# Layer 1 of a fused two-layer kernel: the scaling, shifting and query product of the second half's memory rows move from GpSimd to VectorE, with their operand in a PSUM bank

## The reference, cut to what matters

```
q = l2n(x @ Wq.T);  k = l2n(x @ Wk.T);  v = ln(x @ Wv.T) * vn_g + vn_b
b = sigmoid(xc @ ig_w.T + ig_b) * k * v         # xc: a short convolution of x, through silu
mem[t] = gamma[t] * mem[t-1] + b[t]             # along the tokens
out = (ln(mem) * mn_g + mn_b) * q               # per head     <- the lines that the change moves
o = ln(out) * gn_g + gn_b
y = (o * sigmoid(xc @ og_w.T + og_b)) @ Wo.T
x = x + y + ternary_ffn(x)
```

## Time and profile before

| | |
|---|---|
| median of 3 runs | 904.14 us (903.02 to 904.34) |
| the profiled execution | 904.06 us, of which the span from first to last instruction is 902.3 us |
| TensorE busy (PE) | 752.3 us, 83% of the span |
| VectorE busy (DVE) | 647.4 us, 72% |
| ScalarE busy (ACT) | 451.5 us, 50% |
| GpSimd busy (POOL) | 411.1 us, 46% |
| mean granted TensorE clock | 0.939 of full speed |

### The profile page before, as it was taken

How to read it: one execution, slowest core, us unless ns; L and a number is a source line. 1 busy time by engine, 2 the same in 40 slices (tenths; PEclk the granted TensorE clock), 3 DMA queues, 4 the chain that set the end, 5 groups by cost and what they waited for, 6 DMA issues and landing times. The chain is left out here.

```text
span 902.3 us, 15623 instructions
## 1 busy us (share of the span) xinstructions
PE 752.3 (83%) x5602; PEld 645.9 (72%) x5602; DVE 647.4 (72%) x1146; ACT 451.5 (50%) x717; POOL 411.1 (46%) x335
## 2 busy tenths in 40 slices
PE   3268889999999999999999999990888588595843
PEld 3257678888888888888888888880667376484642
DVE  6998976787777767767777776634548949859765
ACT  4256545655655655655655655553534325335300
POOL 2244542343366585485254254334171743824721
PEclk9999998999999999999999999995889889699785
DMA  5011210210001101101000000004000000000000
GB/s 156 22 42 45 85 36 25 55 37 20 19 21 43 43 20 49 42 20 27 19 3 20 20 3 19 3 1 153 1 1 1 1 24 0 0 23 0 0 23 24
DMA packets 21383, 25.82 MB, mean 29 GB/s; under 512 B 4418, under 2 KB 17090, under 8 KB 21060
## 3 DMA queue, kind: packets, MB, share of 16 engines
q1 hardware_dynamic: 21316, 24.93, 9.4%
HBM read 14.83 MB, written 3.28 MB: 20 GB/s over the span
## 5 line engine op out<-in xcount | busy, mean ns | idle before, releaser
L593 DVE TENSOR_REDUCE neg_max<-s_pair 128x4 f32<-128x1024 f32 x127 | 155.0, 1220 | 80.9 <-PE s_pair L805 80.7
L446 ACT ACTIVATE probs<-t_pair 128x1024 f32<-128x1024 f32 x128 | 131.2, 1025 | 139.5 <-PE t_pair L830 139.1
L345 POOL TENSOR_TENSOR hid<-g,hid 128x512 f32<-128x512 f32 x64 | 82.2, 1284 | 185.5 <-DVE g L704 144.2
L339 POOL TENSOR_TENSOR hid_lo<-hid,hid_hi 128x512 fp32r<-128x512 f32 x64 | 85.8, 1340 | 96.6 <-ACT hid_hi L456 96.5
L805 PE MATMUL s_pair<-K,Q 96*128 96x256 f32 x508 | 85.1, 291 | 15.1 <-DVE neg_max L593 9.7
L805 PEld LDWEIGHTS s_pair<-K,Q 96*128 96x128 f32 x508 | 76.0, 195 | 23.8 <-issue 8.1
L830 PE MATMUL t_pair<-Q,K 104*128 104x512 f32 x256 | 85.6, 416 | 0.3 <-DMA Q<-max_parts 0.3
L872 PE MATMUL down<-w_hi,hid_hi 128*128 128x256 f32 x256 | 83.9, 328 | 0.7 <-POOL hid_lo L339 0.7
L872 PE MATMUL down<-w_lo,hid_hi 128*128 128x256 f32 x256 | 72.1, 282 | 0.0
L872 PE MATMUL down<-w_hi,hid_lo 128*128 128x256 f32 x256 | 72.1, 282 | 0.0
L845 PE MATMUL misc<-probs,V 128*32 128x256 f32 x1024 | 69.6, 390 | 2.0 <-DVE a_mem L570 1.0
(11 more groups left out here) (249 smaller groups left out, 1984.4 us busy)
## 6 DMA issues: line engine op xcount, KB each, us to landing
stage<-in_ternary SPq DMA_DIRECT2D x18, 256.0 KB, 2.8
Q<-q_hi SPq DMA_DIRECT2D x64, 64.0 KB, 2.0
stage<-in_scales SPq DMA_DIRECT2D x8, 384.0 KB, 3.4
X<-in_x SPq DMA_DIRECT2D x8, 256.0 KB, 3.8
Q<-q_lo SPq DMA_DIRECT2D x32, 64.0 KB, 2.0
Q<-max_parts SPq DMA_DIRECT2D x128, 4.0 KB
out<-res SPq DMA_DIRECT2D x8, 256.0 KB, 2.2
shared<-in_l1w SPq DMA_DIRECT2D x1, 1536.0 KB, 6.1
```

The lines of the kernel that those rows point to most:

```text
L339: pool.tensor_tensor(hid_lo[:, m % 2, :, :].rearrange("p a n -> p (a n)"), hid[:, m % 2, :], hid_hi[:, m % 2, :, :].rearrange("p a n -> p ...
L345: pool.tensor_tensor(hid[:, m % 2, :], g[:, m % 2, :], hid[:, m % 2, :], ALU.mult).then_inc(S["hid_done"], 1)
L446: act.activation(probs[:, u % 2, th, :], t_pair[:], ACT.Exp, scale=SCALE).then_inc(S["probs_done"], 1)
L593: dve.tensor_reduce(neg_max[:, u % 2, 4 * jp:4 * jp + 4], score_banks(u, jp)[:].rearrange("p (s n) -> p s n", n=SEQ), AX_X, ALU.max, negat ...
```

## The change

```
@@ memory_scaled: the operand of half 1 is bank 5, no longer `o` in SBUF
-            y = o[:, pair(b), :] if b else turned(banks[4][:])
+            y = turned(banks[4 + b][:])
             inc(linked(engine, wait, f"op_link{b}", [
                 (heads(y), heads(y), mn_g, ALU.mult),
                 (heads(y), heads(y), mn_b, ALU.add),
@@ the queue of GpSimd
-                if late is not None:
-                    memory_scaled(pool, late, 1)
@@ memory_normed: the normed half 1 is written to bank 5 in place
-                        inc(dve.tensor_tensor(heads(o[:, pair(b), :] if b else y), heads(y), each(sm[:, b, :]), ALU.mult), "mn_done")
+                        inc(dve.tensor_tensor(heads(y), heads(y), each(sm[:, b, :]), ALU.mult), "mn_done")
@@ the queue of VectorE
                 if late is not None:
                     memory_scaled(dve, late, 0)
+                    memory_scaled(dve, late, 1)
                 if early is not None:
                     hidden_low(dve, early, 0)
```

## The result

The changed kernel takes 914.87 us (median of 4 runs, 913.95 to 915.72), the kernel before 904.24 beside it; the ratio is 1.012 with a 95% interval of 1.0103 to 1.0138. Forecast were 909.8 us and a range of 906.2 to 912.4. The sign was right, and the cost is nearly twice the forecast one. Timed again later beside other kernels, it took 914.98 us against 904.16.

What follows compares the result with a forecast made beforehand. VectorE's full queue up to `hidden(4)` was taken as the bound: +1.60 us in each of three turns (4.80) plus 0.90 in the last, +5.7 on 904.14, gave 909.8 us (0.6% slower), range 906.2 to 912.4.

Steps and rivals of the forecast that it cites:

- The path: VectorE full up to `hidden(4)`: three added operations cost 2.07 us a turn, net +1.60; GpSimd's relief directly worth zero.
- The credits: On VectorE in the loop's turns, `hidden_low(0)` (L1167) gains 0.09 us and L1508 of half 0 gains 0.38, unstretched by GpSimd.
- The second rival: GpSimd doesn't cause VectorE's stretch, or another of its operations takes the place: no credit, +8.3 us, 912.4 us; chance 0.10.
- The rule that the prediction took: GpSimd shares SBUF interfaces with VectorE; two-SBUF-input instructions contend, so credits are due and the moved operations safe from stretch.
- The last turn: Late part alone, VectorE on the chain to the second `gated`: +2.07 less gains of 1.06 and 0.11, sum +0.90 us.
- The step that failed: On VectorE, L1508 of half 1 stays stretched by GpSimd's `values` of half 0, which moves along; no change counted.
- the two signs of being wrong: VectorE idle between the scans and `hidden(4)`, or `ffn_up(5)` at clock 1.00 in two turns or more.
- The fall of the clock itself: Gap before `ffn_up(3)` grows from 1.54 to 3.1 us; if it then runs slow, it ends 1.8 us later still, off the path.
- The clock behind `hidden(4)`: TensorE's clock effect on the turn's end: zero in the sum, bounds -1.8 and about +0.9 us a turn.
- The first rival: Low clock moves from `ffn_up(5)` to `ffn_up(3)`: -1.8 us a turn; whole 904.4 us, 0.06; one or two turns, 0.18.
- The third rival: TensorE takes over before `hidden(4)`, up to +0.9 us a turn: 911.2 us; chance 0.08.
- the fourth: Rival: freed GpSimd shortens the convolution; price 0, 909.8 us, its chance inside the forecast's 0.58.

Runs made afterwards that it cites:

- e4: The kernel before without the three operations of half 1 on any engine, so the relief of GpSimd alone: 902.07 us (0.9979).
- f3: The changed kernel without the four operations of `values` of half 0 on GpSimd and the waits for it: 907.56 us (1.0038).
- f4: The changed kernel with half 1 kept in bank 5 down to `gated`, centring included: 907.07 us (1.0043).
- e2: The changed kernel with eight extra matmuls on TensorE filling the gap before `ffn_up(3)`: 910.97 us (1.0079).
- e1: The changed kernel with `hidden(2)` moved ahead of the three operations of half 1 on VectorE: 915.39 us (1.0123).
- h1: The changed kernel again, unaltered, timed beside other kernels: 914.98 us (1.0119).
- f2: The kernel before with eight extra matmuls ahead of `ffn_up(3)` and twelve ahead of `ffn_up(5)`: 900.22 us (0.9959).
- g1: The kernel before, bank 6 products of `ffn_up` waiting for ScalarE alone, with four filling matmuls ahead of `ffn_up(3)` and eight ahead of `ffn_up(5)`: 900.40 us (0.995).
- e3: The kernel before with three same-shaped operations more on VectorE, on bank 5, GpSimd keeping its own: 916.27 us (1.0143).
- f1: The changed kernel with eight extra matmuls ahead of `ffn_up(3)` and twelve ahead of `ffn_up(5)`: 905.45 us (1.0009).
- g2: The changed kernel with the split waits and filling of g1 and half 1 centred in bank 5 as in f4: 902.23 us (0.9972).

## Why the prediction was right or wrong

**The path.** Right. VectorE is full between the scans and `hidden(4)` in the changed kernel too, the three operations went on the path whole, and GpSimd's relief was worth nothing directly. In every turn `hidden(3)` came 1.60 us later, the forecast's figure.

**The credits.** Right. L1167 and L1508 of half 0 fell to 0.68 and 0.69 us; e4 has them without the addition. The second rival (no credit, 912.4 us) fell by this, though its price lay nearer to the time. Its clause that another of GpSimd's operations may take the place points the right way, but it was priced at the credited operations alone. The rule that the prediction took from the Trainium skill, "GPSIMD Engine Reference", section "Specifications", agrees with f3 (0.69 us with GpSimd idle) and f4 (0.70 us with one input in a bank).

**The last turn.** Right on VectorE (0.88 us later at the second `gated`, for 0.90), and within 0.15 us at the end of the span (0.75).

**The step that failed** is in the same paragraph as the credits: "L1508 of half 1 is stretched by `values` of half 0, which is not touched and moves along, so I leave it." It didn't move along. `values` of half 0 hangs on the convolution, that on ScalarE's sigmoid behind `ffn_up(3)`, and `ffn_up(3)` lost its clock: GpSimd's operation came 2.7 to 2.9 us later in the turn where VectorE's came 1.6 later. The relative shift of 1.1 to 1.3 us put other pairs side by side, at 1.0 to 1.15 us a turn, 3.2 in all. e2 takes away the low clock and the 3.2 us go with it. Neither of the two signs of being wrong that the prediction named came up: VectorE had no idle time between the scans and `hidden(4)`, and `ffn_up(5)` stayed at the low clock. A busy queue doesn't show that operations in it have grown longer.

The fall of the clock itself had been foreseen, gap of 3.1 us included. Its price was looked for in two places only, at `ffn_up(5)` and in TensorE being late itself, and the chain over ScalarE and GpSimd to the contention was missed, although the same prediction gave credit for contention at another place.

**The clock behind `hidden(4)`** was taken at zero, with bounds of -1.8 (`ffn_up(5)` fast) and +0.9 a turn (TensorE late before it). It was +0.3 to +0.6, 1.4 in all, by a third way: the low clock lasted longer behind `ffn_up(5)`. The first rival (the fast clock moves to `ffn_up(5)`) fell: the gap there was 4.0 to 4.5 us and not 1.5. The stretched operations made `hidden(4)` 1.0 to 1.15 us later still; the low clock delayed `ffn_up(3)` by 1.4 us and not by 1.8; and in the third and fourth turns the products from `gamma(0)` to `gate(1)` took 8.3 to 8.4 us in place of 9.3 to 9.5. Where the stretch was all but absent and `ffn_up(3)` slow (two turns each of f3 and f4), the gap did shrink, to 2.3 us, and `ffn_up(5)` was slow all the same. In e1 and e2 the gap was 3.6 us or more. The third rival (TensorE late) fell by the same gaps. For the fourth, GpSimd idled 9.41 us ahead of the convolution, which came later and not earlier.

**Outside the turns** 1.3 us of the profiled pair weren't forecast. Of these 0.9 lie ahead of the first scan, which is at 680.6 to 684.2 us over the thirteen profiles, with the same code of layer 0 in all; it is at 681.4 in the changed kernel's second profile (h1) and at 680.6 in f4, so this is no effect of the change. The other 0.4 us is found in every run of the kernels with the longer queue, as the last section shows; its cause is open.

The range ended at 912.4, its upper end being a rival that failed. It should have carried the cost of the contention moving.

## What to carry to other kernels

When work is added to a full queue, list what else shifts, and by how much against it: here VectorE's queue behind the addition moved by 1.6 us and GpSimd's `values` by 2.8, and the contention that came of it cost two thirds of the forecast 1.6 us again. A wait of TensorE that is lengthened (here from 1.54 to 3.13 us) should be priced along all that hangs on the matmuls behind it, not at the next critical one alone; filling it with throw-away matmuls is a cheap test, and filling both waits is here also a gain (4 us on the kernel before). A two-input operation of VectorE next to a busy GpSimd wasn't stretched where one of its inputs was in PSUM (f4).

## What the runs showed of the hardware

- An operation with both tensor inputs in SBUF was held up until GpSimd's running instruction was nearly done, whatever its own size: 64 elements took 0.97 us for 0.23, 512 took 1.84 for 0.69. Take from the end of a stretched operation its plain duration, and that of GpSimd's instruction stands 0.14 us behind. L1506 in the second turn: 717.46 + 1.69 - 0.69 = 718.46, and GpSimd's pair ended at 718.60. The small product there: 720.57 + 0.97 - 0.23 = 721.31, and 721.45. L1508 of before: 777.18 + 1.48 - 0.69 = 777.97, and 778.11. From the first scan on, the thirteen profiles have 82 stretched operations (by 0.06 us or more) of four kinds: L1167, the product of k with its norm, the centring and the small product. For all of them the distance is 0.12 to 0.15 us. So the size of a stretch can be read off where the two timelines overlap.
- GpSimd waits as well: where the product was under way first, GpSimd's pair took 3.05 to 3.09 us in place of 2.5. Which of the two waits went by the order of their starts, but for a near tie. Listed 0.12 us ahead of GpSimd's (715.39 against 715.51) the product took 0.72 us; listed 0.02 us ahead (780.52 against 780.54) it took 1.84; and in e2, starting as the first operation of GpSimd's pair ended, 0.69. What decides a near tie stays open.
- The time outside the span is 1.73 to 1.85 us in every run of the kernel before, e4, f2 and g1, and 2.14 to 2.25 us in every run of the changed kernel and of e1, e2, e3, f1, f3, f4 and g2. The second group are the kernels with three more operations in VectorE's turn; matmuls more (f2, g1) or GpSimd operations fewer (e4) make no difference. Why it costs 0.4 us wasn't tried.
- After the same gap of 3.13 to 3.14 us `ffn_up(3)` ran at the low clock in all three turns of the changed kernel and in two of three of f3 and f4, and at the high one in the third turn of each of these two. Nor does the length of a gap settle it elsewhere: the clock was low after 2.3 us (`ffn_up(5)` in two turns each of f3 and f4) and fell within `ffn_up(3)` after 2.2 us (g2); in e4 `ffn_up(5)` began at the high clock after 4.60 us and lost it from its second pair of matmuls on. After the gaps of up to 1.64 us that stood before `ffn_up(3)` and `ffn_up(5)` it was high every time. A forecast for a gap like these should carry both cases.
